# Gated cross-attention block: GpSimd joins the second query tile's probabilities ahead of the row sums, with a new instruction order

## The chip, the cores and the metric

One Trainium2 chip, one of its cores. The metric is the device time of one execution in microseconds, lower is better. The kernel before takes 742.02 us (median of three runs, 741.12 to 743.23).

## What is computed

The block takes x of 16 batches x 256 tokens x 512 and a context of 16 x 256 x 128. It adds gated cross-attention of 16 heads of 32, and then a gated feed-forward part of width 1408 with weights and activations rounded to fp8 steps:

```python
x = x + tanh(g_xattn) * attention(layernorm(x), ctx, Wq, Wkv_expand, Wout)
x = x + tanh(g_ffn) * ffn(layernorm(x), w_gate, w_up, w_down, ...)

# attention: per batch and head
scores = (q @ k.T) / sqrt(32); scores = where(causal, scores, min)
out = softmax(scores) @ v; return out @ Wout.T

# ffn
qx, sx, sc = quantize(x); t = silu(qlinear(qx, w_gate)) * qlinear(qx, w_up)
qt, st, sct = quantize(t); return qlinear(qt, w_down)
```

## The kernel before

A batch has two tiles of 128 tokens (t = 0, 1). Queries, keys and values come from products of high and low bf16 parts. `scores` of pair c of heads (c = 0 to 7; line 891 on) go to PSUM; VectorE takes the row maxima of each (`maxima`, lines 1690 and 1691: 256 elements for the first query tile, 512 for the second). Four short instructions of GpSimd split them (`max_parts`, lines 582 to 585), TensorE turns them (`turned_maxima`), ScalarE copies and a DMA of its queue puts them into the rows of Q4 (`maxima_sent`, line 1319). Then `shifted` (lines 931, 932) makes the transposed, shifted scores, ScalarE their exponentials into a ring PT of 6 pairs (`exps`, line 1338: per head the second key half against the second query tile, and the first key half against both), and GpSimd cuts both causal diagonals (`causal_part`, line 591).

`weighted` (lines 957 and 962) handles group g of four heads: the products of probabilities with V, and the row sums as products with the 0/1 matrix `pick`, both f32, four heads side by side in 32 columns of the array each. For the sums the first key half has 256 query columns and the second, which only the second query tile sees, 128. They add up in one bank (`sum_bank`). `sums_inverted` inverts it, `inverse_spread` writes the inverse to R, `normalised` multiplies, `normalised_high` and `normalised_low` split the result, and `projected` and `residual` end the attention part. R is free from then until the next batch's inverse_spread.

The feed-forward part of a batch runs two or three batches behind in the same stream: `largest_x`, `floored_x`, `lifted_x`, `rounded_x` round the tokens (lines 1722, 1562, 1741, 1558), a transpose DMA turns them, then six chunks n of `gate`/`silu`/`up_scaled`/`up` (lines 1762, 1363, 607, 1779), the maximum and rounding of t (`largest_t` 1786, `floored_t` 1562, `lifted_t` 1804, `rounded_t` 1558), a transpose DMA, `down`, `down_scaled` (1814) and `added` (611), and the store.

Ahead of and among the first batches the weights are made ready: 16 units of w_down, w_gate and w_up (`unit_maxima`, `unit_abs`, `unit_floored`, `unit_lifted`, `unit_rounded` on VectorE or GpSimd, `unit_turned`, `unit_taken`) and ten pieces of the attention's weights (`attention_weights` and its high, exact and low parts). PT, R and x1 hold raw weights in that time.

Each engine has its own program, a loop `for k in range(...)` over steps written out by hand; `at(k + 5, scores, 0)` issues step 0 of batch k + 5 if there is such a batch, and the weights' steps stand in the same loop under `if k == ...`. So the beginning and the end follow the order of the middle with steps left out. Semaphores carry the waits. SP issues the loads, transposes, stackings of keys and queries and the stores in the same way; one step that waits holds all behind it on its queue. Banks of PSUM are given out in tables (`score_pair`, `shifted_pair`, `gate_bank`, ...).

## Time and profile before

| | us |
|---|---|
| median of three runs | 742.02 (741.12 to 743.23) |
| profiled execution, its time | 744.06 |
| its span, first to last instruction | 742.3 |
| TensorE busy (6130 matmuls) | 663.5 |
| VectorE busy | 664.0 |
| ScalarE busy | 552.3 |
| GpSimd busy | 551.3 |

Busy time of an engine is the union of its instructions' times. An instruction that is stalled counts as busy. "Idle before" is the time in which an engine waited ahead of an instruction, with what released it. PE is TensorE's matmuls, DVE VectorE, ACT ScalarE, POOL GpSimd.

### The profile page before, as it was taken

The numbers are of one execution on the slowest core, as the hardware profiler recorded it, in microseconds if no ns is written. First come the engines' busy times: TensorE is split into PE (matmuls) and PEld (weight loads), VectorE is DVE, ScalarE is ACT, GpSimd is POOL, SyncE is SP. The second block draws the span as 40 slices with busy tenths as digits, with TensorE's granted clock in tenths as the row PEclk, the third lists the DMA queues.
The fourth block names the chain that finished last, engine by engine and source line by source line (L and its number), as shares of the span: only waits on it lengthen the run. The fifth ranks groups of instructions, "written<-read, shape, count | busy, mean of one in ns | idle before, by whom it ended". The sixth has DMA issues, their size and how long they took to land.

```text
span 742.3 us, 15885 instructions
## 1 busy us (share of the span) xinstructions
PE 663.5 (89%) x6130; PEld 420.9 (57%) x6130; DVE 664.0 (89%) x1193; ACT 552.3 (74%) x987; POOL 551.3 (74%) x606
## 2 busy tenths in 40 slices
PE   2566889899999999999999999999999999888672
PEld 2445666566666666666565656565666666443220
DVE  6997866989999999899999989898989899998983
ACT  4978779796878787878788787879697959384430
POOL 6577897877878787878879787878787876575341
PEclk9858899999999999999999999999999999999996
DMA  8889776768575666685757565765748565130321
GB/s 288 205 193 165 158 161 106 151 147 155 127 133 115 144 122 135 98 173 92 169 89 157 105 153 112 142 129 129 132 122 137 134 100 133 24 100 16 79 67 48
DMA packets 151208, 95.52 MB, mean 129 GB/s; under 512 B 115326, under 2 KB 121854, under 8 KB 151134
## 3 DMA queue, kind: packets, MB, share of 16 engines
q1 hardware_dynamic: 148974, 92.68, 59.9%
q0 software_dynamic: 576, 1.45, 0.6%
q8 instruction: 48, 0.79, 0.5%
q10 hardware_dynamic: 1584, 0.39, 0.2%
q14 instruction: 26, 0.21, 0.1%
HBM read 31.59 MB, written 9.83 MB: 56 GB/s over the span
## 4 chain that ended last, share of the span: by engine, by line
PE 69%; DVE 12%; ACT 8%; issue 4%; DMA 4%; POOL 2%; SPq 0%; ACTq 0%; POOLq 0%; DVEq 0%
PE pair L730 37%; PE pair L957 6%; PE pair L962 5%; PE pair L932 3%; PE pair L987 3%; PE pair L983 3%; PE pair L988 3%; PE pair L931 2%; PE pair L891 2%; DVE mx L1691 2%; PE pair L893 2%; PE pair L892 2%; DMA PT<-in_L_xattn_Wq_dram 1%; DMA Q<-mT 1%; DVE rsum L1695 1%
## 5 line engine op out<-in xcount | busy, mean ns | idle before, releaser
L607 POOL TENSOR_TENSOR room<-room,up_scale 128x512 f32<-128x512 f32 (+1 forms) x96 | 121.9, 1277 | 43.6 <-ACT room L1363 43.2
L591 POOL TENSOR_SCALAR_AFFINE_SELECT PT<-PT 128x512 f32<-128x512 f32 x128 | 88.0, 700 | 41.6 <-ACT PT L1338 40.7
L1338 ACT ACTIVATE PT<-pair 128x768 f32<-128x768 f32 x128 | 99.8, 810 | 12.8 <-PE pair L962 6.4
L1363 ACT ACTIVATE room<-room,sx 128x512 f32<-128x512 f32 (+1 forms) x96 | 64.9, 679 | 47.3 <-DVE room L1762 47.2
L730 PE MATMUL pair<-WdT,room 128*128 128x512 bf16 x352 | 85.3, 393 | 14.8 <-DMA room<-room 9.8
L730 PE MATMUL pair<-WgT,room 128*128 128x512 bf16 (+1 forms) x384 | 91.3, 361 | 7.0 <-DMA room<-room 3.8
L730 PE MATMUL pair<-WuT,room 128*128 128x512 bf16 (+1 forms) x384 | 91.3, 362 | 1.9 <-DVE room L1762 1.7
L730 PE MATMUL pair<-xT,WqTh 128*128 128x256 bf16 x512 | 88.6, 275 | 1.7 <-ACT exact L1150 1.7
L1691 DVE TENSOR_REDUCE mx<-pair 128x2 f32<-128x512 f32 x128 | 87.3, 682 | 0.0
L1368 ACT ACTIVATE room<-room 128x512 bf16<-128x512 f32 (+1 forms) x96 | 54.7, 586 | 39.6 <-DVE room L1779 38.7
L730 PE MATMUL pair<-xT,WqTl 128*128 128x256 bf16 x256 | 70.5, 275 | 0.0
L730 PEld LDWEIGHTS pair<-WdT,room 128*128 128x128 bf16 x352 | 34.9, 100 | 57.0 <-DMA room<-room 16.9
L611 POOL TENSOR_TENSOR x<-room,x 128x512 f32<-128x512 f32 x32 | 41.3, 1292 | 30.4 <-DVE room L1814 30.4
L1779 DVE TENSOR_TENSOR room<-pair,room 128x512 f32<-128x512 f32 (+1 forms) x96 | 59.9, 638 | 3.2 <-POOL x L611 1.7
L1762 DVE TENSOR_TENSOR room<-pair,gate_scale 128x512 f32<-128x512 f32 (+1 forms) x96 | 60.0, 639 | 2.9 <-PE pair L730 1.3
L891 PE MATMUL pair<-K,Q 125*128 125x128 bf16 x256 | 50.5, 222 | 8.1 <-DMA Q<-kl 4.6
L730 PEld LDWEIGHTS pair<-xT,WqTh 128*128 128x128 bf16 x512 | 49.8, 99 | 13.5 <-ACT exact L1150 2.1
L1804 DVE SCALAR_TENSOR_TENSOR room<-room,tmult 128x1408 f16<-128x1408 f32 x32 | 55.1, 1722 | 0.6
L730 PEld LDWEIGHTS pair<-WgT,room 128*128 128x128 bf16 x384 | 35.4, 98 | 35.2 <-DMA room<-room 4.7
L1690 DVE TENSOR_REDUCE mx<-pair 128x2 f32<-128x256 f32 x128 | 53.5, 418 | 1.8 <-PE pair L893 1.8
L957 PE MATMUL pair<-PT,V 128*32 128x256 f32 (+1 forms) x1024 | 54.7, 331 | 0.0
L962 PE MATMUL pair<-PT,pick 128*32 128x256 f32 (+1 forms) x1024 | 53.4, 326 | 0.0
(137 smaller groups left out, 1902.6 us busy)
## 6 DMA issues: line engine op xcount, KB each, us to landing
xin<-in_x_dram SPq DMA_DIRECT2D x16, 512.0 KB
K<-kh SPq DMA_DIRECT2D x32, 256.0 KB
Q<-qh SPq DMA_DIRECT2D x32, 256.0 KB
x<-in_x_dram SPq DMA_DIRECT2D x16, 512.0 KB, 4.5
out_dram<-x SPq DMA_DIRECT2D x16, 512.0 KB, 3.1
K<-kl SPq DMA_DIRECT2D x16, 256.0 KB
Q<-kl SPq DMA_DIRECT2D x16, 256.0 KB
room<-in_L_ffn_w_down_dram SPq DMA_DIRECT2D x4, 704.0 KB, 7.5
```

The costliest lines, as they stand in the source:

```text
L591: pool.affine_select(out=view, in_=view, compare_op=ALU.is_ge, fill=0.0, base=0, pattern=[[0, 2], [0, 2], [1, P]], channel_multiplier=-1). ...
L607: pool.tensor_tensor(g, g, up_scale[:, chunk(n)[1]], ALU.mult).then_inc(slw_done, 1)
L730: last = pe.matmul(out_ap, lhs, rhs, start=(fresh and n == 0), stop=(n == len(terms) - 1), skip_group_check=not fresh)
L891: pe.matmul(w[:, tok(4 * h)], q[0:MASK_END, head, 0:P], k[0:MASK_END, head, 0:P], start=True, stop=True)
L957: pe.matmul(w[HD * j:HD * j + HD, t * P:S], V[:, t, (G * g + j) * HD:(G * g + j + 1) * HD], probabilities(b, 2 * g + j // 2, j % 2, t), st ...
L962: last = pe.matmul(sum_bank[HD * j:HD * j + HD, t * P:S], pick[:, g, :], probabilities(b, 2 * g + j // 2, j % 2, t), start=(g == 0 and t = ...
L1338: act.activation(head_columns(ring(b, c), 0, 384), head_columns(shifted_pair[c][:, :], 0, 384), ACT.Exp, scale=SCALE).then_inc(exp_done, 1)
L1363: act.activation(g, g, ACT.Silu, scale=sx[:, chunk(n)[0]:chunk(n)[0] + 1]).then_inc(silu_done, 1)
L1691: dve.tensor_reduce(mx[:, heads, 1], head_columns(w, P, 3 * P), AX.X, ALU.max).then_inc(max_done, 1)
L1762: dve.tensor_tensor(gs[:, n % 3, 0:width(n)], gate_bank[n][:, 0:width(n)], gate_scale[:, f], ALU.mult).then_inc(gs_done, 1)
L1779: dve.tensor_tensor(T[:, t, f], up_bank[n][:, 0:width(n)], gs[:, n % 3, 0:width(n)], ALU.mult).then_inc(t_done, 1)
L1804: dve.scalar_tensor_tensor(out=lifted_T[:, t, 0:I], in0=T[:, t, :], scalar=tmult[:, t:t + 1], in1=qt[:, t, :], op0=ALU.mult, op1=ALU.add). ...
```

## The change

1. `joined(b, g)`, new on GpSimd: behind the causal cuts of a group it adds, for four heads, the second key half's 128 columns of probabilities to the first half's columns of the second query tile, into a half of R (`joined_keys`). The row sums of `weighted` then are four products of 128 columns (first query tile) and four of 128 (joined). `weighted` waits for the addition instead of the cuts; additions 3 (and 2 in batch 1) wait for an earlier group's products, since R's halves are used in turn.
2. `maxima` is one reduction of three parts of 128 columns for each of two heads, into an mx of three columns; `second_maxima`, new on VectorE, takes the greater of the last two once a batch, and `max_parts` waits for it. The scales of the weights are multiplied column by column.
3. Every engine's order is new. Beginning and end are written out step by step, and a loop is left for eight batches in the middle (`for k in range(1, 9)`). Waits are set per step and batch where the order doesn't imply them.
4. The tables of PSUM banks are new.

```diff
-        mx = sb("mx", [P, NH, TT])
+        mx = sb("mx", [P, NH, TT + 1])
...
+        def joined_keys(g):
+
+            return R[:, g % 2 * 2:g % 2 * 2 + 2, :].rearrange("p a (h s) -> p (a h) s", h=2)
...
-        v_bank = (bank[1], bank[7])
+        v_bank = (bank[0], bank[7])
...
-        shifted_pair = (pairs[2], pairs[0], pairs[3], pairs[2], pairs[1], pairs[2], pairs[0], pairs[2])
-        turn_bank = bank[2]
-        weighted_bank = (bank[3], bank[5])
+        shifted_pair = (pairs[2], pairs[0], pairs[2], pairs[2], pairs[0], pairs[2], pairs[0], pairs[2])
+        turn_bank = bank[3]
+        weighted_bank = (bank[3], bank[4])
...
-                pool.wait_ge(max_done, 8 * b + 8)
-                m = mx[:, :, :].rearrange("p h t -> p (h t)")
+                pool.wait_ge(max_joined, b + 1)
+                m = mx[:, :, 0:TT]
...
+            def joined(b, g):
+                pool.wait_ge(cut_done, 8 * b + 2 * g + 2)
+                if g == 2 and b == 1:
+                    pool.wait_ge(group_made, 5)
+                if g == 3:
+                    pool.wait_ge(group_made, 4 * b + 2)
+                first = (NC * b + 2 * g) % RING
+                heads = PT[:, first:first + 2, :].rearrange("p c n -> p (c n)").rearrange("p (h n) -> p h n", h=G)
+                pool.tensor_tensor(joined_keys(g), heads[:, :, 0:P], heads[:, :, 2 * P:3 * P], ALU.add).then_inc(join_done, 1)
...
+            for k in range(1, 9):
...
+                causal_part(k + 2, 0)
+                causal_part(k + 2, 1)
+                causal_part(k + 2, 2)
+                joined(k + 2, 0)
+                added(k - 1, 1)
+                causal_part(k + 2, 3)
+                causal_part(k + 2, 4)
+                causal_part(k + 2, 5)
+                joined(k + 2, 1)
+                causal_part(k + 2, 6)
+                causal_part(k + 2, 7)
+                joined(k + 2, 2)
+                joined(k + 2, 3)
+                queries_low(k + 3, 1)
...
             def weighted(b, g):
...
+                pe.wait_ge(join_done, 4 * b + g + 1)
...
-                for t in range(TT):
-                    for j in range(G):
-                        last = pe.matmul(sum_bank[HD * j:HD * j + HD, t * P:S], pick[:, g, :],
-                                         probabilities(b, 2 * g + j // 2, j % 2, t), start=(g == 0 and t == 0),
-                                         stop=(g == KT - 1 and t == TT - 1), skip_group_check=True)
+                for j in range(G):
+                    first = probabilities(b, 2 * g + j // 2, j % 2, 0)[:, 0:P]
+                    pe.matmul(sum_bank[HD * j:HD * j + HD, 0:P], pick[:, g, :], first, start=(g == 0), stop=(g == KT - 1),
+                              skip_group_check=True)
+                for j in range(G):
+                    last = pe.matmul(sum_bank[HD * j:HD * j + HD, P:S], pick[:, g, :], joined_keys(g)[:, j, :], start=False,
+                                     stop=(g == KT - 1), skip_group_check=True)
...
-                dve.tensor_reduce(mx[:, heads, 0], head_columns(w, 0, P), AX.X, ALU.max)
-                dve.tensor_reduce(mx[:, heads, 1], head_columns(w, P, 3 * P), AX.X, ALU.max).then_inc(max_done, 1)
+                dve.tensor_reduce(mx[:, heads, :], head_columns(w, 0, 3 * P).rearrange("p h (r s) -> p h r s", s=P), AX.X,
+                                  ALU.max).then_inc(max_done, 1)
+
+            def second_maxima(b):
+                dve.wait_ge(max_done, 8 * b + 8)
+                dve.tensor_tensor(mx[:, :, 1], mx[:, :, 1], mx[:, :, 2], ALU.max).then_inc(max_joined, 1)
```

The order of TensorE around the sums, from `turned_maxima` of batch b to the next batch's scores, in the middle of the kernel. Before: turned_maxima(b), gate(b-2, 4), up(b-2, 2), queries(b+1, 2), gate(b-2, 5), queries(b+1, 3), projected(b-1, 2), shifted(b, 0), shifted 1, down(b-3, 1), shifted 2, projected(b-1, 3), shifted 3, up 3, shifted 4, up 4, shifted 5, shifted 6, weighted 0, up 5, shifted 7, weighted 1, 2, 3, values(b+1, 0), values 1, down(b-2, 0), gate(b-1, 0). After: turned_maxima(b), gate(b-2, 4), gate(b-2, 5), up(b-2, 2), projected(b-1, 2), queries(b+1, 2), shifted(b, 0), projected(b-1, 3), shifted 1, queries(b+1, 3), shifted 2, down(b-3, 1), shifted 3, 4, up 3, shifted 5, weighted 0, shifted 6, up 4, shifted 7, values(b+1, 0), up 5, weighted 1, values 1, weighted 2, 3, down(b-2, 0), up(b-1, 0), gate(b-1, 0). Around the maxima ScalarE has silu(b-2, 2), maxima_taken, silu(b-2, 3), maxima_sent, where before silu(b-2, 2), queries_high, silu(b-2, 3), maxima_taken and maxima_sent followed one another. At the start SP loads unit 0, unit 1, x of batch 0, w_kv, the context, unit 3, w_q, unit 2; before it was unit 0, unit 1, w_kv, unit 2, w_q, unit 3, the context, x. At the end VectorE does the last `floored_t(15, 0)`, three ups, `largest_t(15, 1)`, `lifted_t(15, 0)`, `floored_t(15, 1)`, `rounded_t(15, 0)`, `lifted_t(15, 1)`, `rounded_t(15, 1)`, where it rounded the first tile wholly ahead of the three ups.

## Rows read from the trace of the kernel before

**Rows 1.** The page: busy time, share, instructions; the chain of waits by engine.
```profile
PE 663.5 (89%) x6130; PEld 420.9 (57%) x6130; DVE 664.0 (89%) x1193; ACT 552.3 (74%) x987; POOL 551.3 (74%) x606
...
PE 69%; DVE 12%; ACT 8%; issue 4%; DMA 4%; POOL 2%; SPq 0%; ACTq 0%; POOLq 0%; DVEq 0%
```

**Rows 2.** Busy by stretch: length, PE, PEld, DVE, ACT, POOL; clock, DMA share, GB/s.
```profile
399.20:437.80 38.60, 38.60 (x377) 24.45 (x371) 36.38 (x71) 31.47 (x59) 31.19 (x35) 1.00 0.64 130
70.10:102.40 32.30, 27.84 (x314) 21.30 (x315) 23.04 (x44) 24.45 (x43) 28.77 (x31) 0.86 0.73 161
102.40:135.20 32.80, 28.89 (x341) 20.51 (x342) 26.16 (x56) 27.57 (x51) 26.94 (x33) 1.00 0.68 132
135.20:172.70 37.50, 36.69 (x360) 23.32 (x360) 33.90 (x69) 31.98 (x60) 30.84 (x36) 1.00 0.78 159
172.70:636.80 464.10, 463.50 (x4428) 293.59 (x4429) 436.55 (x828) 372.42 (x683) 368.08 (x403) 1.00 0.64 128
636.80:742.30 105.50, 73.15 (x475) 34.49 (x474) 85.51 (x144) 41.98 (x73) 49.61 (x46) 0.91 0.21 56
```

**Rows 3.** Timelines of GpSimd and VectorE: start, length, instruction, idle before.
```profile
81.03 0.21 POOL L584 CAST m_parts<-m_rest 128x32 bf16<-128x32 f32 x1
...
416.23 1.59 POOL L584 CAST m_parts<-m_rest 128x32 bf16<-128x32 f32 x1
...
416.07 1.68 DVE L1804 SCALAR_TENSOR_TENSOR room<-room,tmult 128x1408 f16<-128x1408 f32 x1
```

**Rows 4.** Timelines of VectorE and GpSimd in the weights' preparation.
```profile
43.17 5.26 DVE L1562 TENSOR_SCALAR room<-room,wmult 128x512 bf16<-128x512 bf16 x2
...
43.79 4.21 POOL L541 TENSOR_TENSOR room<-room 128x1024 bf16<-128x1024 f32 x2
...
54.45 1.79 DVE L1678 SCALAR_TENSOR_TENSOR room<-room,wmult 128x512 f32<-128x512 f32 x2
```

**Rows 5.** Timeline of VectorE and, last, of GpSimd in one batch.
```profile
405.94 0.42 DVE L1690 TENSOR_REDUCE mx<-pair 128x2 f32<-128x256 f32 x1
406.27 0.68 DVE L1691 TENSOR_REDUCE mx<-pair 128x2 f32<-128x512 f32 x1
406.87 0.42 DVE L1690 TENSOR_REDUCE mx<-pair 128x2 f32<-128x256 f32 x1
...
408.73 0.42 DVE L1558 TENSOR_TENSOR room<-cx,room 128x512 bf16<-128x512 f16 x1
...
432.76 0.35 DVE L1562 TENSOR_SCALAR room<-room,xmult 128x512 bf16<-128x512 bf16 x1
...
434.72 0.41 DVE L1558 TENSOR_TENSOR room<-cx,room 128x512 bf16<-128x512 f16 x1
...
435.01 0.64 POOL L591 TENSOR_SCALAR_AFFINE_SELECT PT<-PT 128x512 f32<-128x512 f32 x1 [0.35 <-ACT PT L1338]
```

**Rows 6.** One batch by line: length, VectorE busy (lines 1562, 1558, 1804, 1741 in turn).
```profile
399.20:437.80 38.60, 2.24 (x4) 1.00 0.64 130
399.20:437.80 38.60, 2.60 (x4) 1.00 0.64 130
399.20:437.80 38.60, 3.36 (x2) 1.00 0.64 130
399.20:437.80 38.60, 1.76 (x3) 1.00 0.64 130
```

**Rows 7.** Timeline of TensorE: one group's sums and what follows.
```profile
435.75 0.83 PE L962 MATMUL pair<-PT,pick 128*32 128x256 f32 x16
436.40 0.83 PE L957 MATMUL pair<-PT,V 128*32 128x256 f32 x16
```

**Rows 8.** Groups by line and shape, 200 to 640 us: count, busy us, mean ns, idle.
```profile
L607 POOL TENSOR_TENSOR room<-room,up_scale 128x512 f32<-128x512 f32 x44 | 56.1, 1276 | 29.7 <-ACT room L1363 29.7
L597 POOL TENSOR_TENSOR ol<-R,oh 128x512 bf16<-128x512 f32 x24 | 27.8, 1158 | 10.7 <-ACT oh L1150 10.7
```

**Rows 9.** Timeline of TensorE at the end: the last down and its wait.
```profile
732.08 4.87 PE L730 MATMUL pair<-WdT,room 128*128 128x512 bf16 x11 [9.00 <-DMA room<-room]
```

## What the change is expected to do

> **What bounds the kernel now.** I read the page first, for the share of each engine in 40 slices; then the busy times by stretch, for the length of a batch; then the timelines of one batch on TensorE, VectorE and GpSimd, laid over one another. The page [rows 1] has TensorE at 89% and GpSimd at 74% over the whole span, which alone names no bound. The stretches do [rows 2]: from 172.7 us, where the scores of batch 3 begin, to 636.8 us, where those of batch 15 begin, TensorE is busy 463.5 of 464.1 us at a granted clock of 1.00. Twelve batches pass there, 38.67 us each; an undisturbed one takes 38.63 us, the length of eleven of the twelve between the starts of their scores. In such a batch VectorE is busy 36.4, ScalarE 31.5 and GpSimd 31.2 us [rows 2]. The chain of waits is TensorE for 69% [rows 1]. So in the middle TensorE's work sets the time. Ahead of 172.7 us and behind 636.8 us it does not: the three starting stretches show TensorE busy 27.8 of 32.3, 28.9 of 32.8 and 36.7 of 37.5 us, the end 73 of 105.5 us [rows 2].
>
> Of GpSimd's 31.2 us not all is work. Its cast of 128x32 takes 0.21 us at 81.03 us and 1.59 us at 416.23 us, where VectorE's scalar_tensor_tensor of line 1804 runs from 416.07 to 417.75 us; the cast ends when that one does [rows 3]. It happens the other way round too: at 43.17 us two tensor_scalar of VectorE take 5.26 us together while GpSimd runs two subtractions of 4.21 us back to back [rows 4]; one of that size takes 0.35 us at 432.76 us [rows 5]. So VectorE's lines 1804, 1741, 1558 (two inputs in SBUF) and 1562 (bf16 to bf16) do not run at the same time as an instruction of GpSimd: whoever is second waits. I call them the excluding instructions. There are 12 in a batch, busy 10.0 us (3.36, 1.76, 2.60 and 2.24 us by line) [rows 6]. Reductions, the products out of PSUM and the shuffles lie beside GpSimd's work without a trace of it. The Trainium skill (SBUF — State Buffer, Who interferes with whom) says that the shared port pair is locked for a whole instruction by a VectorE instruction in a two-port mode, and against a GpSimd instruction that reads SBUF by one with two SBUF inputs, and that the other one fully blocks. By that rule, the trace agrees, in both directions; taken to the letter it gives the sum below, and if a good part of an instruction were free of the lock it would give the first rival's.
>
> **How much room that leaves.** In the batch at 399.2 to 437.8 us GpSimd is idle 38.6 - 31.2 = 7.4 us. Excluding instructions fill part of it: five places, from 0.41 us at 408.73 to 0.29 us at 434.72, where GpSimd's next cut begins at 435.01 [rows 5], 2.4 us together, and 0.2 us in the gaps of GpSimd's short chains, 2.6 us in all. In 4.8 us of each batch neither GpSimd nor an excluding instruction runs. That is the room for new GpSimd work.
>
> **The change, part by part.** *Row sums.* A group of the sums is 16 records on TensorE: 8 of 256 columns and 8 of 128, in 0.65 us from one group's start to the next instruction's (435.75 to 436.40 us) [rows 7]. Afterwards all 16 are of 128 columns, so two thirds of the columns are left: 0.43 us. That saves 0.217 us a group, 0.87 us a batch, and TensorE's batch becomes 37.8 us. The row doesn't part the two kinds; if a narrow record took as long as a wide one the saving would be 0, so it lies between 0 and 0.87 us. I take the latter, as TensorE's other products go by columns.
>
> *The additions.* Four on GpSimd a batch, each 128x512 f32 from two f32 operands. The nearest row, line 607 with the same shape and types, has 1.28 us [rows 8]. That is 5.1 us; less the 0.03 us by which neighbours overlap, 5.0 us. Bounds: 1.16 us, as line 597 with a bf16 output [rows 8] (4.6 us a batch), and 1.48 us, if each meets a quarter of an excluding instruction of 0.9 us (5.9 us). I take 5.0. Queued behind each on GpSimd stand the next causal cuts, and the products of TensorE now wait for the addition instead of the cut; the last two cost 2.5 us behind the last cut, which the schedule covers with values (1.3 us), the last up product (0.65) and group 1 (1.1). If that cover is gone, the cost is up to 2.5 us a batch.
>
> *Maxima.* Two reductions of 0.33 and 0.60 us from start to start (405.94, 406.27, 406.87 us) [rows 5] become one of 768 elements. 256 elements more cost 0.26 us (0.42 to 0.68), so it takes 0.94 us and 0.87 from start to start, for 0.93: eight times, -0.5 us. The joining of the second halves is a new instruction with two inputs in SBUF, priced by no row of its size; the difference between 0.42 us for 256 elements and their 0.26 leaves 0.16 us. It is itself excluding: if GpSimd is in keys_low it waits up to 1.2 us. Between -0.4 and +0.8 us of VectorE; taken at 0, as it isn't the bound. max_parts, turned_maxima and the DMA of the maxima wait behind it. On TensorE the new order leaves one quarter of the queries less (12 products, 1.3 us) between turned_maxima and the first shifted product, and on ScalarE maxima_sent now stands behind one more silu (0.7 us). 0 to 1.5 us a batch, taken at 0: TensorE has to idle elsewhere anyhow, as follows.
>
> *The middle.* 5.0 us of additions meet 4.8 us of room: 38.63 + 5.0 - 4.8 = 38.8 us with no moment left unused. Some stays unused, for GpSimd's queue is in order and waits for silu and exp 14 times a batch. I take 0.8 us, a sixth of the present 4.8 (ends: 0, and 3 us if the pattern of waits hardly tightens). A batch of 39.6 us, +1.0 over 38.63; 12 batches, +12 us (ends: +2 and +38).
>
> *The beginning.* The written-out order turns fewer weight units ahead of the first scores: units 8 and 9 are floored and lifted later, keys of batch 0 no longer queue behind unit_turned(4), which waits for GpSimd's unit_rounded(4) (the first of the two subtractions at 43.79 us) [rows 4], x of batch 0 is loaded ahead of w_kv, and SP is passed by load_x1 and the mask loads. The first scores could come at 58 instead of 70.1 us: VectorE is through with unit 7 at 56.2 us [rows 4]. But that work isn't gone, it comes between scores 0 and 3, where GpSimd is busy 28.8 of 32.3, 26.9 of 32.8 and 30.8 of 37.5 us [rows 2] and the excluding instructions of the units (line 1562 and 1678) come on top. Laid over one another, they and GpSimd leave 2.7, 1.4 and 5.0 us free there, 9 in all, and the three batches bring 15 us of additions. I take +4 us for the scores of batch 3 (ends: -10, all of the early start kept; +12).
>
> *The end.* 105.5 us from the scores of batch 15. VectorE is busy 85.5 [rows 2]; the last down waits 9 us for floored, lifted, rounded and the transpose of the last tile [rows 9]. There the new order moves the first tile's rounding behind the last ups and the second tile's maximum ahead. GpSimd has room here. -2 us for the order, 0 for the additions (ends: -6, +3).
>
> *Sum.* The profiled execution spans 742.3 us (its time is 744.06; the median of three is 742.02, so I count the change from 742.0): 742.0 + 12 + 4 - 2 = 756 us.
>
> **The rivals.** *The exclusion doesn't bind (faster).* The additions find GpSimd's idle time, the rounding falls into ScalarE's waits, TensorE stays without gaps at 37.8 us: 12 x -0.86 = -10 us, the start keeps -8, the end -2: 722 us. For it: TensorE has no gap now, and GpSimd's 28 instructions, each at the least its kind shows, are some 27.4 us and with the additions 32.5, under 37.8. Against: with the 10.0 us of excluding instructions it is 42, of which the batch may run at once only what it does today at small chains, some 1.4 us, besides stalls already counted. It decides from there: if more than 1 us a batch beyond today's runs at once, it is this case. *The order fits the exclusion.* A batch of 38.8 us, the start -4, the end -2: 742 + 2 - 6 = 738; with the start at 0 it is 742. *VectorE starves.* With GpSimd at 97% each of 12 excluding instructions waits half of a 1.2 us instruction: VectorE's 35.9 us become 42; 12 x 3.5 = 42, with the start 790 us. Against it: today the waits are under 0.7 us a batch. *The change doesn't do what it says*: if a narrow record of the sums takes as long as a wide one, TensorE gains nothing, and all the additions cost is cost; the time is the forecast's, since there TensorE isn't what binds.
>
> **How the numbers follow.** Forecast (748 to 768 us) 0.47; the exclusion doesn't bind 0.17; the order fits 0.20, half of it below 739.8 us, a third within, the rest above; starving or longer waits, over 768 us, 0.16. 0.3% is 2.2 us, about what a measurement of this kernel can tell from no change. Faster 0.17 + 0.10 = 0.27, same 0.07, slower 0.66. The range leaves out half of the first rival and half of the starving one: 727 to 774 us.
>
> **What would show it.** In the changed kernel's middle: the batch at 39.6 us and TensorE with about 1.8 us of waits in it, most for GpSimd's additions or for VectorE; GpSimd busy over 36 us a batch; lines 1562 and 1741 busy more than 2.2 and 1.8 us a batch [rows 6]; four additions of 1.27 to 1.5 us; the sums at 0.43 us a group. First scores near 58 us and those of batch 3 near 177 us. Wrong it is if TensorE has no gaps and the batch is 37.8 us: then the excluding instructions ran beside GpSimd's longer than I think, or fell where it waits.

## The result, and the profile after

The changed kernel takes 823.62 us (median of four runs, 818.83 to 826.97) beside 742.62 (741.12 to 743.26) of the kernel before in the same comparison: ratio 1.1089, interval 1.103 to 1.1148. The forecast had the sign right and the size far too small: 756 us, with a range that ended at 774. The profiled execution took 823.87 us, its span is 822.1, against 742.3.

The page of the changed kernel: busy times (of before in [rows 1]), the chain of waits by engine, and the groups of the additions and of the cuts (line engine operation, count | busy, mean ns | idle before).

```profile
PE 671.1 (82%) x6051; PEld 416.4 (51%) x6130; DVE 704.9 (86%) x1099; ACT 554.1 (67%) x987; POOL 651.2 (79%) x670
...
POOL 35%; DMA 15%; DVE 14%; ACT 11%; PE 10%; SPq 8%; issue 5%; POOLq 0%; DVEq 0%
...
L809 POOL TENSOR_SCALAR_AFFINE_SELECT PT<-PT 128x512 f32<-128x512 f32 x128 | 109.5, 879 | 7.7 <-ACT PT L2251 7.3
...
L820 POOL TENSOR_TENSOR R<-PT 128x512 f32<-128x512 f32 x64 | 89.8, 1411 | 0.8
```

The chain was TensorE's for 69% [rows 1]; now TensorE has 10% of it and GpSimd 35%, and the load of the context is on it. TensorE sets the time almost nowhere any more. The stretches (columns as in [rows 2]):

```profile
61.20:106.60 45.40, 31.57 (x359) 26.23 (x362) 36.62 (x59) 32.33 (x51) 36.33 (x36) 0.82 0.67 143
106.60:142.50 35.90, 30.45 (x330) 21.44 (x333) 27.55 (x44) 26.46 (x50) 32.63 (x37) 0.90 0.61 108
142.50:186.80 44.30, 37.84 (x354) 23.46 (x360) 36.77 (x57) 31.51 (x58) 40.28 (x44) 0.96 0.60 136
186.80:528.80 342.00, 310.15 (x2916) 191.93 (x2956) 314.68 (x498) 253.48 (x465) 298.33 (x304) 1.00 0.61 118
528.80:720.10 191.30, 161.39 (x1453) 96.97 (x1474) 163.16 (x253) 120.81 (x220) 144.32 (x147) 0.96 0.59 103
720.10:822.10 102.00, 72.98 (x466) 34.72 (x473) 83.50 (x133) 42.03 (x74) 55.21 (x50) 0.90 0.26 58
```

They are cut at the first scores of batches 0, 1, 2, 3, 11 and 15. The scores of batch 3 come 14.1 us later (186.8, before 172.7). The eight batches from 3 up to the scores of 11 take 42.75 us each, where before every batch took 38.6: +32 us. The last four take 47.8 each: +37. The tail is 3.5 us shorter (102.0, before 105.5). The sum is the 79.8 us between the spans. Two causes must be told apart: the additions, and the order.

### The profile page after: what moved, and what is told of

Read it like the earlier page. It is cut to its first block, busy times and chain, and to the rows that moved or that the text cites. A ratio compares the mean times of both kernels' runs of the same rounds, so it can differ in the third digit from the quotient of the medians.

```text
span 822.1 us, 15621 instructions
## 1 busy us (share of the span) xinstructions
PE 671.1 (82%) x6051; PEld 416.4 (51%) x6130; DVE 704.9 (86%) x1099; ACT 554.1 (67%) x987; POOL 651.2 (79%) x670
## 4 chain that ended last, share of the span: by engine, by line
POOL 35%; DMA 15%; DVE 14%; ACT 11%; PE 10%; SPq 8%; issue 5%; POOLq 0%; DVEq 0%
POOL PT L809 10%; POOL R L820 8%; PE pair L1200 5%; POOL room L836 5%; SPq L403 4%; POOL kl L779 4%; DVE mx L3050 4%; DMA cin<-in_ctx_dram 4%; DMA Q<-mT 3%; DMA xT<-xcat 2%; POOL x L845 2%; DVE room L3199 2%; POOL rstd L722 2%; POOL xcat L741 2%; ACT xcat L2116 2%
## 5 line engine op out<-in xcount | busy, mean ns | idle before, releaser
L3050 DVE TENSOR_REDUCE mx<-pair 128x6 f32<-128x768 f32 x128 | 117.5, 950 | 14.3 <-PE pair L1384 13.8
L809 POOL TENSOR_SCALAR_AFFINE_SELECT PT<-PT 128x512 f32<-128x512 f32 x128 | 109.5, 879 | 7.7 <-ACT PT L2251 7.3
L1200 PE MATMUL pair<-WdT,room 128*128 128x512 bf16 x338 | 82.9, 395 | 14.6 <-DMA room<-room 12.4
L1200 PE MATMUL pair<-WuT,room 128*128 128x512 bf16 (+1 forms) x366 | 88.1, 363 | 7.3 <-DMA room<-room 3.1
L1200 PE MATMUL pair<-xT,WqTh 128*128 128x256 bf16 x512 | 90.6, 279 | 3.6 <-ACT exact L2015 2.2
L820 POOL TENSOR_TENSOR R<-PT 128x512 f32<-128x512 f32 x64 | 89.8, 1411 | 0.8
L1422 PE MATMUL pair<-Q,K 99*128 99x128 bf16 x256 | 49.0, 223 | 15.8 <-DMA Q<-mT 13.6
L3290 DVE SCALAR_TENSOR_TENSOR room<-room,tmult 128x1408 f16<-128x1408 f32 x32 | 58.7, 1834 | 0.1
```

The costliest lines, as they stand in the source:

```text
L809: pool.affine_select(out=view, in_=view, compare_op=ALU.is_ge, fill=0.0, base=0, pattern=[[0, 2], [0, 2], [1, P]], channel_multiplier=-1). ...
L820: pool.tensor_tensor(joined_keys(g), heads[:, :, 0:P], heads[:, :, 2 * P:3 * P], ALU.add).then_inc(join_done, 1)
L1200: last = pe.matmul(out_ap, lhs, rhs, start=(fresh and n == 0), stop=(n == len(terms) - 1), skip_group_check=not fresh)
L3050: dve.tensor_reduce(mx[:, heads, :], head_columns(w, 0, 3 * P).rearrange("p h (r s) -> p h r s", s=P), AX.X, ALU.max).then_inc(max_done, 1)
L3290: dve.scalar_tensor_tensor(out=lifted_T[:, t, 0:I], in0=T[:, t, :], scalar=tmult[:, t:t + 1], in1=qt[:, t, :], op0=ALU.mult, op1=ALU.add). ...
```

## The experiments

In the comparisons the median of the kernel before lies between 742.6 and 744.1 us. A "batch" is the time from the first scores of one batch to those of the next, in the profiled execution. "Stalls" below are worked out over all VectorE instructions of a stretch, as what each lasted beyond the shortest of its shape in the same run; in the kernel before they are 1.2 to 1.3 us a batch.

**The order and the additions apart.** First the changed kernel without the additions (the products of the row sums go back to those of the kernel before as well, not shown in the cut):

```diff
             def joined(b, g):
-                pool.wait_ge(cut_done, 8 * b + 2 * g + 2)
...
-                pool.tensor_tensor(joined_keys(g), heads[:, :, 0:P], heads[:, :, 2 * P:3 * P], ALU.add).then_inc(join_done, 1)
+                pass
...
-                pe.wait_ge(join_done, 4 * b + g + 1)
+                pe.wait_ge(cut_done, 8 * b + 2 * g + 2)
```

> The changed kernel without the additions: the four additions a batch are gone, the row sums are made of the probabilities as in the kernel before (eight products of 256 and eight of 128 columns, the products waiting for the cuts), and order, banks and maxima stay as changed. Three theories of the 81 us. A, the additions' time on GpSimd: a batch of the middle falls by about 4 us to TensorE's 38.6, and with the ends the kernel comes to 745 to 760 us. B, the new order by itself is the loss: the middle stays at 42 to 43 us a batch and the time at 805 to 825 us. C, both in part: the middle goes to 38.6 to 39.5 us a batch, but the last three batches ahead of the ending (46.9, 51.4 and 49.2 us from scores to scores, with GpSimd busy 30.8 of the last one's 49.2 us) stay some 7 us a batch too long: 765 to 785 us. I hold C.

It took 790.33 us, ratio 1.0631 (1.0609 to 1.0652): the order, the banks and the maxima alone cost 46 us. Its batches from 3 to 11 take 40.1 us, 39.8 in the steady part; batches 11 to 15 take 41.8, 43.0, 46.9 and 50.1 from scores to scores; batch 3 comes at 182.9; the tail is 98.9 us. In the terms of my sum, from the profiled run: start +10, eight batches +11, the last four +27, tail -7. Theory C is right in kind, both causes are there, and the last batches went as it said. But the middle is longer than its 38.6 to 39.5 us, and with that and the start, which C had left out, the time lies above its range. A and B, each as the whole cause, are out.

Then the changed kernel with the additions cut to 8 of 128 columns, all waits kept:

```diff
-                pool.tensor_tensor(joined_keys(g), heads[:, :, 0:P], heads[:, :, 2 * P:3 * P], ALU.add).then_inc(join_done, 1)
+                pool.tensor_tensor(joined_keys(g)[:, :, 0:8], heads[:, :, 0:8], heads[:, :, 2 * P:2 * P + 8], ALU.add).then_inc(join_done, 1)
```

> The changed kernel with each addition cut to 8 of its 128 columns a head (the other columns of the joined sums are left out): every instruction, wait and place stays, only the 1.27 to 1.44 us of each addition shrink to some 0.1 us. A, the time that GpSimd is taken up: as without additions at all, within 1 per cent of that kernel. If instead the wait of the products for the additions is what costs (theory D: the cut's signal to GpSimd, the addition and its signal to TensorE, in series), this one stays close to the changed kernel, 800 to 825 us, while the kernel without additions is fast. B, the order: 805 to 825 us for both.

788.45 us, 1.0564 (1.0513 to 1.0615), which overlaps the kernel without additions. So what the additions cost goes with their length on GpSimd's queue, not with the signal that they put between cut and product. Theory D is out.

The reverse, the kernel before with the four additions and nothing else changed:

```diff
                 at(k + 2, causal_part, 2)
+                at(k + 2, joined, 0)
...
                 at(k + 2, causal_part, 5)
+                at(k + 2, joined, 1)
...
                 at(k + 2, causal_part, 7)
+                at(k + 2, joined, 2)
+                at(k + 2, joined, 3)
```

> The kernel before with the four additions alone: its own order, banks and maxima, each addition placed as in the changed kernel (behind cuts 2, 5, 7 and 7), the sums made of the joined columns. A, the additions' time on GpSimd beside VectorE's excluding instructions: 5.0 us more work in 7.4 us of idle time, of which 2.6 are taken by excluding instructions; if the unused time stays at 4 us as in the changed kernel's loop, a batch takes about 42.5 us and the kernel 742 + 13 x 3.9 = 793 us, plus some at the start: 785 to 805. My forecast's sum with 0.8 us unused gives a batch of 39.6 and 754 to 758 us. B, the order is the loss: 738 to 750 us here.

812.14 us, 1.0913 (1.0885 to 1.0942), a batch of 42.7 us. So the additions alone cost 68 us in the old order (812.1 - 744.1), and 33 of the changed kernel's 81 in its own (824 - 790). The two costs don't add up: 68 for the additions and 46 for the order, each alone, are more than the 81 of both together. My sum (39.6 us a batch) is refuted without any change of order, and so is theory B. The time lies above theory A's 805, its batch of 42.5 us was close.

**A wait that GpSimd's queue makes elsewhere.** In the changed kernel the context's load is issued last on SP's queue, behind steps that wait for GpSimd's steps after the additions. Moved ahead (with it goes a wait for the buffer to be free):

```diff
                 stack_keys(k + 4, 2)
+                load_c(k + 6)
...
-                load_c(k + 6)
```

> The changed kernel with one DMA issue moved: in the loop of eight batches the context's load is issued on SP's queue behind the third stacking of the keys, 13 issues earlier than at the loop's end, with a wait for GpSimd's c_low that frees its buffer. Theory E: the middle's 42.6 us are a ring of waits, from GpSimd's queries_low and x_low behind the additions over SP's stackings of the queries to the context's load (5.1 us), ScalarE's c_high and means, back to GpSimd's scales of the next batch. If so, c_high's wait for the context (16.5 us over six batches) goes and a batch gets 1 to 3 us shorter, 8 to 24 us in all: 800 to 815 us. Theory A, GpSimd's own time with what VectorE excludes is the bound, and the load is late only because everything is: the wait moves to another place and the time stays within 0.5 per cent of the changed kernel's.

813.99 us, 1.0945 (1.0927 to 1.0963): 10 us less, a batch of 41.0 to 41.5 us, and ScalarE's wait for the context (14.2 us in six batches of the changed kernel) is gone from its waits. Theory E holds, for 1.3 us of the batch. What is left reads like a ring, a chain of waits that comes back to its own start one batch later. GpSimd, then VectorE, in one batch of this kernel (start, length, instruction, idle before):

```profile
376.49 3.22 POOL L809 TENSOR_SCALAR_AFFINE_SELECT PT<-PT 128x512 f32<-128x512 f32 x3
379.67 1.90 POOL L820 TENSOR_TENSOR R<-PT 128x512 f32<-128x512 f32 x1
381.53 1.34 POOL L845 TENSOR_TENSOR x<-room,x 128x512 f32<-128x512 f32 x1
382.81 2.47 POOL L809 TENSOR_SCALAR_AFFINE_SELECT PT<-PT 128x512 f32<-128x512 f32 x3
385.26 1.26 POOL L820 TENSOR_TENSOR R<-PT 128x512 f32<-128x512 f32 x1
386.47 1.23 POOL L809 TENSOR_SCALAR_AFFINE_SELECT PT<-PT 128x512 f32<-128x512 f32 x2
387.67 2.56 POOL L820 TENSOR_TENSOR R<-PT 128x512 f32<-128x512 f32 x2
...
417.65 2.03 POOL L809 TENSOR_SCALAR_AFFINE_SELECT PT<-PT 128x512 f32<-128x512 f32 x1
```

```profile
391.64 1.76 DVE L3059 RECIPROCAL rsum<-pair 128x256 f32<-128x256 f32 x1 [0.87 <-PE pair L1456]
...
396.67 0.95 DVE L3050 TENSOR_REDUCE mx<-pair 128x6 f32<-128x768 f32 x1
...
406.22 0.18 DVE L3055 TENSOR_TENSOR mx<-mx 128x16 f32<-128x16 f32 x1
```

From the first cut to the last addition 13.7 us without a gap on GpSimd (376.5 to 390.2); to the sums' inverse 1.4 (the last group's products); to the end of normalised and the first maximum of the next batch 5.0; the maxima 9.5; their parts 1.7; turning, the DMA of the maxima, shifted, exponentials and the next first cut 9.8. Together 41.2 us, the batch (any chain of steps from one first cut to the next adds up to that; what speaks for a ring is which of its parts move). Without the additions GpSimd's stretch is 9.1 us (405.5 to 414.5 in that kernel) and the inverse comes 4.75 us behind the last cut, 3.3 more than the 1.4 of above: that is the slack which the additions' 4.6 us used up first.

The old order shows it more plainly. The kernel before, then the same with four additions: first cut, last cut or addition, inverse, and the next batch's first cut:

```profile
428.21 1.33 POOL L591 TENSOR_SCALAR_AFFINE_SELECT PT<-PT 128x512 f32<-128x512 f32 x2 [1.37 <-ACT PT L1338]
436.23 0.64 POOL L591 TENSOR_SCALAR_AFFINE_SELECT PT<-PT 128x512 f32<-128x512 f32 x1 [0.58 <-ACT PT L1338]
439.25 1.76 DVE L1695 RECIPROCAL rsum<-pair 128x256 f32<-128x256 f32 x1 [0.44 <-PE pair L962]
466.85 1.34 POOL L591 TENSOR_SCALAR_AFFINE_SELECT PT<-PT 128x512 f32<-128x512 f32 x2 [1.37 <-ACT PT L1338]
```

```profile
464.94 1.34 POOL L596 TENSOR_SCALAR_AFFINE_SELECT PT<-PT 128x512 f32<-128x512 f32 x2 [1.36 <-ACT PT L1359]
476.65 1.51 POOL L605 TENSOR_TENSOR R<-PT 128x512 f32<-128x512 f32 x1 [0.16 <-PE pair L984]
479.57 1.76 DVE L1716 RECIPROCAL rsum<-pair 128x256 f32<-128x256 f32 x1 [2.28 <-PE pair L984]
507.41 1.33 POOL L596 TENSOR_SCALAR_AFFINE_SELECT PT<-PT 128x512 f32<-128x512 f32 x2 [1.36 <-ACT PT L1359]
```

From first cut to last cut or addition 8.7 and 13.2 us; from there to the inverse 2.4 and 1.4; from the inverse to the next first cut 27.6 and 27.8. Only the stretch of the cuts has grown, by 4.6 us, the wait ahead of the inverse gave up 1.0 of it, and the rest of the way is as long as before: 42.5 us instead of 38.6.

**Is it the ring, or GpSimd's time?** The kernel before with four additions of the same size whose result nobody reads, outside the stretch from first cut to sums:

```diff
+            def spare_added(b):
+                if 1 <= b <= 14:
...
+                    pool.tensor_tensor(R[:, 0:2, :], R[:, 2:4, :], R[:, 2:4, :], ALU.add).then_inc(spare_done, 1)
...
                 at(k + 3, keys_low, 1)
+                at(k + 1, spare_added)
...
                 at(k, up_scaled, 3)
+                at(k + 1, spare_added)
...
                 at(k + 4, scales1)
+                at(k + 1, spare_added)
...
                 at(k, added, 0)
+                at(k + 2, spare_added)
```

> The kernel before, plus four more instructions of GpSimd a batch (batches 2 to 14) with the size and type of the additions (128x512 f32 from two f32 operands, on R while nobody needs it), whose result nobody reads, and whose places are outside the stretch from the first cut to the products of the sums: behind keys_low, up_scaled(3), scales1 and added(k, 0). Theory F: the batch is a ring of waits, first cut, last cut or addition, weighted, inverse, normalised, the next batch's maxima, their DMA, shifted, exponentials, first cut; the additions cost what they lengthen of it, less 1.0 us of slack. Then GpSimd's 5.0 us a batch cost nearly nothing here: a batch of 38.6 to 39.3 us, 742 to 751 us. Theory A: GpSimd's time together with what VectorE excludes is the bound; then it costs as much as the additions did in the old order, a batch of 42 to 43 us, 790 to 812 us.

758.61 us, 1.0206 (1.0188 to 1.0224), 39.8 us a batch: 1.2 us, where the same work among the cuts costs 4.1. Place makes most of the price. Theory A is far off, and F's "nearly nothing" (742 to 751 us) was wrong too. With the two at the widest holes alone (behind scales1 and added(k, 0)):

> The kernel before with two more instructions of GpSimd a batch (batches 2 to 14), of the additions' size, at the two places where GpSimd waits longest in it: behind added(k, 0) (2.09 us of idle time follow) and behind scales1 (1.37 us). The result is read by nobody. With four such instructions the batch took 39.8 us. Theory G: what an instruction costs is what it sticks out of the idle time at its place and what queues behind it; these two lie in holes, 2.5 us a batch cost nothing: 742 to 746 us, a batch of 38.6 to 38.7. Theory A: cost goes by GpSimd's time, half of the four's: 750 to 752 us, a batch of 39.2.

756.88 us, 1.0187 (1.0166 to 1.0208), 39.8 us a batch: the same price for half of the work. Neither G nor A. VectorE's stalls rose from 1.2 to 3.6 us a batch here, and to 2.5 with four.

Then theory F's other use, to shorten the ring under the four additions. up_scaled(k, 5) moves ahead of the first cut, and lifted_t(k - 2, 1) behind up(k - 1, 0), so that GpSimd's cast of [rows 3] isn't held up:

```diff
                 at(k + 4, scales1)
+                at(k, up_scaled, 5)
...
-                at(k - 2, lifted_t, 1)
                 at(k - 1, up, 0)
+                at(k - 2, lifted_t, 1)
```

> The kernel before with the four additions as in the run of the old order, and two moves that take other work off the ring while all work stays: up_scaled(k, 5) stands behind scales1, ahead of the first cut, not behind the third (0.97 us), and VectorE's lifted_t(k - 2, 1) stands behind up(k - 1, 0), so that it no longer holds up GpSimd's cast of the maxima (1.59 us, where it takes 0.21 alone). Theory F: the ring gets 0.97 + 1.3 us shorter, the batch goes from 42.7 to 40.4 us, the kernel from 812 to 780 to 784 us. Theory A: GpSimd's work is the same; only the stall of the cast, 1.4 us, is gone from its busy time: the batch between 41.3 and 42.7 us, 794 to 812 us.

> The kernel before with the two moves alone (up_scaled(k, 5) ahead of the first cut, lifted_t(k - 2, 1) behind up(k - 1, 0)), no additions. Theory F: the ring is 2.3 us shorter, but it already had 1.0 us of slack beside TensorE's 38.63 us of work, so the time stays: 740 to 744 us, a batch of 38.6 us. If the ring were what sets the batch in the kernel before, it would fall by up to 2 us a batch (715 to 735 us).

With additions 796.48 us, 1.0725 (1.0703 to 1.0747), 41.6 us in most batches, 41.8 on average; without them 746.47, 1.0047 (1.0031 to 1.0063), 38.6. With additions that is half of what F said, and it lies inside theory A's ranges, so this run doesn't speak for F. Without them the batch is F's 38.6 us, while the time is 2.5 us above its range; the ring doesn't set the batch of the kernel before. With additions the stretch of the cuts got 1.3 us shorter (13.2 to 11.9), the batch 1.1. The cast took 0.21 us, the maxima's parts 1.2 instead of 2.6, and the way from there to the first cut got 1.4 us longer in both kernels: it is not the parts that come last there but ScalarE's queue, where the copy of the turned maxima stands behind two silus and a copy that wait for VectorE. The stall of [rows 3], with which I showed the exclusion, costs nothing where it stands. From the inverse to the next batch's first maximum the moves even added 0.6 us (5.9 instead of 5.3).

**Fewer additions.** Group 0 alone (at its place of above); groups 0 and 1 with both moves; groups 1 and 2, with up_scaled moved, placed so:

```diff
                 at(k + 2, causal_part, 4)
+                at(k + 2, joined, 1)
...
                 at(k + 2, causal_part, 6)
+                at(k + 2, joined, 2)
```

> The kernel before with the addition of group 0 alone, behind the third cut as in the changed kernel, and no moves: the dose of one to the run with four. Theory G: it is ahead of TensorE's products of group 0, which stand ahead of shifted 7, and it delays all later cuts by 1.25 us less the 0.9 us that GpSimd waits for exponentials at the last two: the batch becomes 39.3 to 39.9 us (slack 1.0 us in the path to the sums, none in the path over shifted 7), 750 to 758 us. Theory A, cost in proportion to the additions' time: a quarter of 4.1 us less 0.2 of TensorE: 39.5 us, 753 us. The two don't part here; what parts from both is my forecast's room of 4.8 us, by which one addition is free and the batch 38.4 us, 739 to 742 us.

> A version meant to beat both: the kernel before with the additions of groups 0 and 1 alone (the other two groups' sums as before) and the two moves. Theory F: the ring is 37.65 us without additions and slack, +2.0 to 2.5 for two additions, -2.3 for the moves, 37.4 to 37.9 us, and TensorE's work is 38.63 - 2 x 0.217 = 38.2 us, which is then the bound: 38.2 us a batch, 735 to 739 us. Theory A: 2.5 us more of GpSimd in a batch cost about half of the four additions' 4.1 us: 40 to 40.7 us a batch, 762 to 770 us.

> A version meant to beat both: the kernel before with additions for groups 1 and 2 alone, placed behind cuts 4 and 6, so that TensorE's products of group 0, which stand ahead of shifted 7, wait for no addition (in the run with groups 0 and 1 that wait was 11.7 us over ten batches), and up_scaled(k, 5) ahead of the first cut, so that the last cut comes no later than before. TensorE's work is 38.63 - 2 x 0.217 = 38.2 us. Theory G (place decides): TensorE stays the bound, 38.2 to 38.4 us a batch, 736 to 741 us. Theory A (GpSimd's time decides): 2.5 us more cost some 0.6 to 2 us a batch less 0.4: 745 to 765 us.

761.19 us, 1.0241 (1.0217 to 1.0266), 39.6 us a batch; 767.21, 1.0319 (1.0296 to 1.0342), 40.0; 768.76, 1.0358 (1.0331 to 1.0385), 40.2. One addition costs 1.0 us a batch, where my room of 4.8 us made it free (739 to 742 us); G had its batch right (39.3 to 39.9), and its time 3 us too low. For two, F (735 to 739 us) and G (736 to 741) fail. Theory A had the first (762 to 770 us) and is 4 us low on the second (745 to 765). Neither of the two versions meant to beat both does, nor did any other run. One batch of the kernel with one addition and of that with groups 1 and 2:

```profile
415.20:454.80 39.60, 38.28 (x365) 24.30 (x370) 37.83 (x70) 31.47 (x59) 32.54 (x35) 1.00 0.65 127
```

```profile
417.50:457.70 40.20, 38.20 (x366) 24.21 (x371) 39.11 (x70) 31.53 (x58) 33.71 (x36) 1.00 0.62 125
```

TensorE is busy less (38.3 and 38.2 us instead of 38.6, the sums' saving is real), VectorE more: 37.8 and 39.1 us, where it was 36.4 [rows 2]. That is stalls, 3.0 and 4.3 us a batch. In the kernel with one addition (250 to 630 us, some ten batches) TensorE waits 8.7 us for VectorE and for no addition; in that with groups 1 and 2 it waits 9.7 us for VectorE and 6.0 for additions. This is a cost that neither F nor G has, and it goes over VectorE.

**Who has room?** Four reductions of 128x512 from SBUF more on VectorE, a kind that takes no longer beside GpSimd's additions (below):

```diff
+                    dve.tensor_reduce(spare[:, i:i + 1], down_scale[:, :], AX.X, ALU.max)
```

> The kernel before with four more reductions of VectorE a batch (batches 2 to 14; 128x512 f32 from SBUF, a kind that GpSimd doesn't stop, some 0.6 us each from start to start, 2.4 us in all), read by nobody. It measures VectorE's room. Theory H: VectorE is nearly a second bound, with about 1.0 us a batch to spare, so the batch becomes 38.6 + 2.4 - 1.0 = 40.0 us, 759 to 762 us. If its 2.2 us of idle time could all be used: 38.8 us, 744 to 746 us. If it has no room at all, 41 us, 773 us.

769.88 us, 1.0374 (1.0343 to 1.0404), 41.0 us in most batches and 40.7 on average: 2.4 us of work cost 2.1 to 2.4, and the stalls rose to 2.4 us in most batches. VectorE has hardly any usable room, though its row shows 2.2 idle us a batch; H's 1.0 us was still too much. It is a second bound beside TensorE.

And GpSimd memsets, which read nothing, first at the places outside the cuts, then in the places of the additions, the sums made as before. TensorE waits for them as for the additions; GpSimd's own waits for TensorE's earlier groups are left out:

```diff
-                    pool.tensor_tensor(R[:, 0:2, :], R[:, 2:4, :], R[:, 2:4, :], ALU.add).then_inc(spare_done, 1)
+                    pool.memset(R[:, :, :].rearrange("p k s -> p (k s)").bitcast(BF16)[:, 0:1408], 0.0).then_inc(spare_done, 1)
...
-                pool.tensor_tensor(joined_keys(g), heads[:, :, 0:P], heads[:, :, 2 * P:3 * P], ALU.add).then_inc(join_done, 1)
+                pool.memset(R[:, :, :].rearrange("p k s -> p (k s)").bitcast(BF16)[:, 0:1408], 0.0).then_inc(join_done, 1)
```

> The kernel before with four GpSimd memsets a batch (1408 bf16 elements of R, 1.27 us in the run of the exclusion alone for a memset of that many) at the places of the four additions off the cuts' stretch, results read by nobody. It parts the two ways in which those additions can have cost 1.2 us a batch. Theory H: VectorE's instructions with two inputs in SBUF stall behind an addition (its stalls rose from 1.2 to 2.5 us a batch), and VectorE has only some 1 us a batch to spare beside TensorE. A memset reads nothing; if it doesn't lock VectorE out, VectorE's stalls stay at 1.2 us and the batch at 38.6 to 38.8: 742 to 745 us. Theory K, GpSimd's queue in order: what stands behind comes later, whatever the instruction is: 39.8 us a batch, 757 us. If a memset locks VectorE out like an addition, the time is 757 us too, but with the stalls.

> The kernel before with such a memset in the place of each of the four additions between the cuts, with the same waits of GpSimd and of TensorE for it, and the sums made as before (so TensorE's work is 38.63 us, not 37.8). The stretch from first cut to last memset gets 4.6 us longer, as with the additions; VectorE isn't locked out, if a memset doesn't do that. Theory F, for what four additions cost beyond two: the path over the cuts, sums, maxima, shifted and exponentials is a ring whose slack is 1.0 us, so the batch becomes 38.65 - 1.0 + 4.6 = 42.2 us, 795 to 805 us. Theory H alone (only VectorE's stalls cost): 38.6 to 39 us, 742 to 748 us.

761.33 us, 1.0248 (1.0216 to 1.028), 39.96 us a batch; and 803.18, 1.0831 (1.0795 to 1.0868), 42.2 us. The first kernel shows VectorE's instructions with two inputs in SBUF beside a memset:

```profile
417.33 1.27 POOL L600 MEMSET R<- 128x1408 bf16 x1
417.63 0.41 DVE L1571 TENSOR_TENSOR room<-cx,room 128x512 bf16<-128x512 f16 x1
...
424.18 1.27 POOL L600 MEMSET R<- 128x1408 bf16 x1
...
424.98 1.67 DVE L1817 SCALAR_TENSOR_TENSOR room<-room,tmult 128x1408 f16<-128x1408 f32 x1
```

Two excluding instructions of VectorE begin beside it and take their shortest times, 0.41 and 1.67 us. The other kind, the bf16 tensor_scalar, is held out by a memset. It meets none in batches 3 to 10 of either kernel, but it does at the start of the second (GpSimd's cuts and memset, then VectorE):

```profile
128.74 1.79 POOL L596 TENSOR_SCALAR_AFFINE_SELECT PT<-PT 128x512 f32<-128x512 f32 x2
130.49 1.26 POOL L603 MEMSET R<- 128x1408 bf16 x1
...
129.96 1.94 DVE L1579 TENSOR_SCALAR room<-room,xmult 128x512 bf16<-128x512 bf16 x1
```

It takes 0.35 us at its shortest; here it ends at 131.90, just behind the memset (131.75). In the middle, then, no memset held VectorE out. And still the batch outside the cuts costs 1.3 us as with additions, and VectorE's stalls are 2.5 us a batch as with additions. So theory H's forecast (742 to 745 us) fails and K's 39.8 us is close: it is not the new instruction's own lock. It shifts what stands behind it on GpSimd's queue, and the old instructions then meet VectorE's excluding ones for longer: the rounding of t (128x1408, f16 to bf16) is stalled 0.5 us a batch here and hardly at all in the kernel before. Between the cuts four such memsets cost 3.6 us a batch, F's number (42.2), with no lock of theirs: it is the length that they add to the ring. (In this kernel TensorE's granted clock falls as well behind its waits for them, to 0.51 in one slice of 3 us. The inverse comes 1.6 us behind the last memset in most batches and 2.1 to 2.6 in the others, so in some batches up to 1.0 us is the clock's.)

Last, the same two kernels with additions and 4.0 us a batch less on VectorE:

```diff
-                dve.tensor_reduce(amax[:, t:t + 1], cx[:, t, :], AX.X, ALU.max, apply_absolute_value=True).then_inc(amax_done, 1)
+                dve.tensor_reduce(amax[:, t:t + 1], great[:, :], AX.X, ALU.max, apply_absolute_value=True).then_inc(amax_done, 1)
...
-                dve.tensor_reduce(tm[:, t:t + 1], T[:, t, :], AX.X, ALU.max, apply_absolute_value=True).then_inc(tmax_done, 1)
+                dve.tensor_reduce(tm[:, t:t + 1], great[:, :], AX.X, ALU.max, apply_absolute_value=True).then_inc(tmax_done, 1)
```

> The run with four additions outside the cuts' stretch, with less work on VectorE: its four large reductions for the rounding scales (largest_x twice, 0.60 us, largest_t twice, 1.53 us from start to start) read eight constants instead (the scales, and so the feed-forward's values, are left out), which takes 4.0 us a batch off VectorE; all instructions and waits stay. Theory H, VectorE is the second bound that the stalls push beyond TensorE: the batch returns from 39.8 to TensorE's 38.6 us, 741 to 746 us. Theory K, what stands behind in GpSimd's queue comes late: GpSimd's work is the same, 39.8 us, 755 to 759 us.

> The run of the old order with the four additions between the cuts, with the same 4.0 us a batch taken off VectorE (the scales left out). Theory F, four additions lengthen the ring over the cuts, which goes through VectorE's inverse, normalised and maxima but not through the reductions that are gone: the batch stays at 41.7 to 42.7 us, 795 to 812 us. Theory H alone, VectorE's stalls are the whole cost: back to 38.0 to 39 us, 735 to 750 us.

750.21 us, 1.0101 (1.0079 to 1.0123), 39.2 us a batch, between the two theories: half of the 1.2 us goes with VectorE's work, and what makes the other half no run shows. And 822.23 us, 1.1049 (1.0986 to 1.1112), 44.3 us a batch, above both theories: the kernel is even 10 us slower than the one with VectorE's full work. Slices of 3 us of that kernel where TensorE waits for an addition and then makes the products (first column of numbers TensorE's busy time, the fifth GpSimd's, then the granted clock):

```profile
475.80:478.80 3.00, 3.00 (x49) 1.99 (x47) 2.42 (x5) 2.85 (x6) 3.00 (x4) 1.00 0.81 234
478.80:481.80 3.00, 0.68 (x17) 0.43 (x20) 2.94 (x6) 3.00 (x6) 3.00 (x5) 1.00 0.63 210
481.80:484.80 3.00, 1.43 (x36) 0.83 (x28) 0.71 (x3) 2.74 (x6) 3.00 (x3) 0.60 0.05 11
484.80:487.80 3.00, 3.00 (x52) 2.27 (x48) 0.00 (x0) 0.00 (x0) 3.00 (x4) 0.50 0.02 5
```

TensorE waits 2.3 us, makes one group's products, waits 1.6 us, and its clock falls from 2.4 to 1.2 GHz just for the last two groups' products, which are on the ring: the inverse comes 3.4 us behind the last addition instead of 1.4. Without these 2.0 us the batch would be 42.3, so relief on VectorE brings next to nothing between the cuts, as F said. With VectorE's full work the clock falls there too, for a shorter time (0.83 and 0.60 in two slices, 16 of TensorE's products 1.51 us instead of 0.86): the inverse comes 1.4 us behind the last addition in some batches (42.5 us) and 2.1 in others (42.9). Of the 4.1 us that four additions cost there, a few tenths are the clock's. In the middle of the changed kernel the granted clock is 1.00.

**The maxima alone.**

```diff
-                dve.tensor_reduce(mx[:, heads, 0], head_columns(w, 0, P), AX.X, ALU.max)
-                dve.tensor_reduce(mx[:, heads, 1], head_columns(w, P, 3 * P), AX.X, ALU.max).then_inc(max_done, 1)
+                dve.tensor_reduce(mx[:, heads, :], head_columns(w, 0, 3 * P).rearrange("p h (r s) -> p h r s", s=P), AX.X,
+                                  ALU.max).then_inc(max_done, 1)
...
                 at(k + 1, maxima, 7)
+                at(k + 1, second_maxima)
```

> The kernel before with the change of the maxima alone: one reduction of 768 elements for each pair of heads, second_maxima behind the eighth, and max_parts waiting for it. My forecast took it at nothing (between -0.4 and +0.8 us a batch of VectorE, which was not taken for a bound). Theory H: VectorE's work falls by 0.3 us a batch, which TensorE's bound hides; the joining lies in the path of the maxima, 0.2 us: 740 to 745 us, a batch of 38.6 us.

745.39 us, 1.0026 (1.0006 to 1.0046), 38.6 us a batch in most: by its interval between nothing and 0.5% slower.

**The exclusion by itself.** A kernel of its own; the core of each phase:

```python
for n in range(N - 1):
    step(n)
step(N - 1).then_inc(dve_at, 1)
dve.wait_ge(dve_at, 2 * phase)
for n in range(N - 1):
    step(n)
```

> A kernel of its own that measures the exclusion (nothing of the block is computed, the output is zeros). Eight kinds of VectorE instruction, each six times back to back alone, and then six times while GpSimd does six additions of the changed kernel's form (128x512 f32, 4 x 128 columns out of PT). By the forecast's premise lifted (scalar_tensor_tensor, two inputs in SBUF, 128x1408), floored (bf16 tensor_scalar), rounded (two inputs in SBUF) and the product of two f32 operands in SBUF never run beside an addition: the two engines' times add up, six additions and six instructions take the sum of both. Reductions from SBUF and PSUM, the product of PSUM with SBUF and the shuffle run beside it at full speed, and the addition stays at 1.27 us. If the exclusion were only partial, the first four pairs would end earlier than the sum of their times.

GpSimd's timeline (start, length of the six additions), in the order of the phases: alone; then beside lifted, floored, rounded, a reduction from SBUF, one from PSUM, the product with PSUM, the product of two SBUF operands, the shuffle:

```profile
10.29 7.36 POOL L73 TENSOR_TENSOR R<-PT 128x512 f32<-128x512 f32 x6 [0.82 <-DVE pair L114]
27.58 15.71 POOL L73 TENSOR_TENSOR R<-PT 128x512 f32<-128x512 f32 x6 [9.93 <-DVE f_out L89]
46.60 9.11 POOL L73 TENSOR_TENSOR R<-PT 128x512 f32<-128x512 f32 x6 [3.32 <-DVE b_out L93]
60.86 11.23 POOL L73 TENSOR_TENSOR R<-PT 128x512 f32<-128x512 f32 x6 [5.15 <-DVE b_out L96]
81.59 7.39 POOL L73 TENSOR_TENSOR R<-PT 128x512 f32<-128x512 f32 x6 [9.50 <-DVE most L99]
94.59 7.36 POOL L73 TENSOR_TENSOR R<-PT 128x512 f32<-128x512 f32 x6 [5.62 <-DVE most L102]
105.88 7.38 POOL L73 TENSOR_TENSOR R<-PT 128x512 f32<-128x512 f32 x6 [3.93 <-DVE f_out L105]
117.55 9.70 POOL L73 TENSOR_TENSOR R<-PT 128x512 f32<-128x512 f32 x6 [4.29 <-DVE f_out L108]
129.68 7.38 POOL L73 TENSOR_TENSOR R<-PT 128x512 f32<-128x512 f32 x6 [2.44 <-DVE f_out L111]
```

This is one execution. Six lifted alone take 9.8 us (17.77 to 27.58), and beside six additions both take 15.7 together, 1.5 less than the sum. Floored takes 3.2 alone, 9.1 with the additions' 7.4; rounded 5.0 and 11.2; two f32 operands in SBUF 4.2 and 9.7. The other four leave the additions at 7.4 us. So the premise holds, up to the 0.2 to 0.3 us by which two such instructions overlap.

## Why the forecast was wrong, step by step

- *The middle, +12.* It was +69: +32 in the eight batches of the loop and +37 in the four before the end. Two steps failed. The first is "how much room that leaves", and the sentence that 5.0 us of additions meet 4.8 us of room. Idle time of GpSimd was taken as a stock from which work can be paid wherever it stands. It isn't: in the order of the kernel before, the additions alone make the batch 42.7 us where this sum has 39.6; four memsets, which held VectorE out nowhere in the middle, cost 3.6 us a batch between the cuts and 1.3 elsewhere; and two additions in the widest holes cost as much as four. The second is the new order, "0 to 1.5 us a batch, taken at 0": without the additions 38 of the 69 us are there (11 in the loop, 27 in the four batches), and the additions bring the other 31.
- *The luck in it.* The sign was right and its reason, the additions' time on GpSimd, was one of the two causes. The size was not: 823.6 lies beyond the 790 of the worst rival, in the branch "over 768 us" that had a chance of 0.16, and beyond the 795 us that the sum gives with its own worst ends for the middle, start and end.
- *What I took for the bound.* "In the middle TensorE's work sets the time" was true and half of it. VectorE was a second bound with hardly anything to spare (four more reductions cost nearly their whole time), and the ring over cuts, sums, maxima and exponentials was a third with 0.8 us of slack: in the kernel before the inverse comes 2.4 us behind the last cut and 1.55 behind the start of the last group's products. (The theories above count 1.0, with the 1.4 that the narrower joined sums need.) [rows 2] could not show either: a stretch without a gap on TensorE says which engine is bound, not how far behind it the next chain is. The sentence "the last two cost 2.5 us behind the last cut, which the schedule covers" was the place to follow that chain round to the next batch.
- *The exclusion.* The premise was right, for GpSimd's instructions that read; its way to the cost was another than in my sum. VectorE, the second bound, is stalled 3.0 us a batch with one addition and 4.4 in the changed kernel, where it was 1.2. How much of the changed kernel's time that makes was not measured. The excluding lines did grow: lines 2891 and 3138 of the changed kernel are busy 2.93 and 3.10 us in the batch at 444.2 us, where 1562 and 1741 had 2.24 and 1.76 [rows 6]. The rival "VectorE starves" had the better batch (42 us) by that route, but partly by luck: VectorE's busy time in that batch is 38.8, not 42, and 4.0 us less of VectorE's work brought back 0.6 us outside the cuts and next to nothing between them.
- *The row sums.* The size of a product was right: the eight narrow ones that were wide take 0.22 us instead of 0.43. But from a group's sums to the next instruction, the measure of [rows 7], it is mostly 0.55 us and not 0.43 (480.75 to 481.31 in the changed kernel), for the next group, which now has a wait of its own, starts some 0.12 us later than the usual step between products. TensorE's busy time fell by 0.2 to 0.3 us a joined group. Since TensorE no longer is the bound, it is worth nothing.
- *The additions.* Four instructions, 5.67 us in that batch, 1.41 us on average: inside the bounds of 4.6 and 5.9, above the 5.0 taken. The cuts, which I left as they were, grew from 700 to 879 ns on average.
- *The maxima.* One reduction has 0.95 us, 0.94 was said, and the join 0.18 (0.16). Taken at 0; the run with it alone gives 2 us for the kernel, up to 3.4 by its interval.
- *What the order does.* I priced it only at the ends. In the middle it stood in the sum at nothing. By itself it costs 1.2 us in most batches of the loop (VectorE's stalls there are 3.0 instead of 1.2 us, and TensorE waits), 1.3 more for the context's load once GpSimd is late, and 27 us in the four written-out batches ahead of the end.
- *The beginning, +4 (-10 to +12).* +14. The first scores came at 61.2 us (58 was said), and as foretold the work isn't gone: the first batch took 45.4 us instead of 32.3. It is +10 without the additions, and in the old order with them +13, so either alone makes most of it, and the term was too small for both.
- *The end, -2 (-6 to +3).* -3.5, but right in part by luck: without the additions it is -6.6, so the order brought more than 2 us and the additions, taken at 0, cost 3 (one profiled execution of each).
- *The signs.* TensorE waits some 4 us in the batch at 444.2 us, not 1.8, about half of it for the additions. GpSimd is busy 38.0 us (over 36 was said). The scores of batch 3 came at 186.8 us (177).

TensorE's waits in the six batches from 230 to 486.9 us (waiting line, released by: us in total, times, longest):

```profile
PE pair L1448 <- POOL R L820: 12.5, 16, 1.3
PE pair L1200 <- ACT exact L2015: 4.8, 5, 1.7
PE pair L1479 <- DVE mx L3050: 2.6, 6, 0.5
```

What stays open: why the new order by itself costs 46 us, above all which step of the written-out last batches makes them 42 to 50 us long. In the kernel without additions TensorE waits there for a transposed tile (5.5 us once), ScalarE for values (13.7 us once), and I made no experiment on it. How the half of 1.2 us that doesn't go with VectorE's work arises, in the run with additions outside the cuts, was not followed further either.

## What to carry to other kernels

Before work is put into the idle time of an engine, follow the loop-carried chain once around a period, and write down the slack of each segment; work on the chain costs its length less that slack (four additions lengthen the stretch of the cuts by 4.6 us and have 1.0 to use up; 4.1 were measured), whatever the engine's share. An idle share, even a hole of 2 us at the very place, is no price: the queue behind it shifts, and the old instructions then meet others than before. Measure the room of each engine with a dummy instruction before the real one is built.

## What the runs showed of the hardware

- Exclusion of GpSimd's additions and VectorE's instructions with two SBUF inputs (or bf16 tensor_scalar): 15.7 us for both where the sum is 17.2, so all but 0.2 to 0.3 us of each instruction. Beside a reduction, an operand in PSUM or a shuffle six additions take their 7.4 us. The Trainium skill (SBUF — State Buffer, Who interferes with whom) says that such instructions fully block one another; the trace agrees, but for that overlap.
- A GpSimd memset of 1408 elements (1.27 us) does not hold out VectorE's instructions with two SBUF inputs: 0.41 and 1.67 us beside one, their shortest times. It does hold out a bf16 tensor_scalar: 1.94 us instead of 0.35.
- TensorE's granted clock fell to 1.2 GHz (0.50) behind waits of 2.3 and 1.6 us with one group's products between them, within an otherwise full batch, and the last group's products, which were on the chain, took 2.4 us instead of 1.4 up to the inverse. Here TensorE's waits were so paid twice.
